# Prenorm attention with a two-layer local transformer branch: local scores in blocks of 64 queries by 128 keys, and one set of output transposes

## The reference

```
h = shift_token(x)                  # second half of the features comes from the token before
q, k, v = split(h @ wqkv)           # 8 heads of 64
q, k = l2norm(q) * qs, l2norm(k) * ks ; rotary embedding with a scale, q also times 8
# queries in blocks of 64; block w sees the keys of blocks w - 1 and w
mask = (i < j) | (i > j + 64) | (j == -1)
o = softmax(q k^T, masked) @ v
x = x + o @ wo
h = layernorm(shift_token(x)) * lg + lb
x = x + ((a * gelu(g)) @ w2 + b2)   # a, g = split(h @ w1 + b1), 341 features each
```

## Time and profile before

| | us |
|---|---|
| median of 3 runs | 3053.88 |
| lowest and highest | 3053.64, 3055.64 |
| the profiled execution's own time | 3055.99 |
| its span, first to last instruction | 3054.2 |
| busy in it: TensorE matmuls (PE) | 2986.4 (98%) |
| VectorE (DVE) | 1993.5 (65%) |
| ScalarE (ACT) | 1662.5 (54%) |
| GpSimd (POOL) | 1014.3 (33%) |

### The profile page before, as it was taken

How to read it: one execution, slowest core, us unless ns; L and a number is a source line. 1 busy time by engine, 2 the same in 40 slices (tenths; PEclk the granted TensorE clock), 3 DMA queues, 4 the chain that set the end, 5 groups by cost and what they waited for, 6 DMA issues and landing times.

```text
span 3054.2 us, 87852 instructions
## 1 busy us (share of the span) xinstructions
PE 2986.4 (98%) x34560; PEld 2067.3 (68%) x34560; DVE 1993.5 (65%) x6942; ACT 1662.5 (54%) x3126; POOL 1014.3 (33%) x987
## 2 busy tenths in 40 slices
PE   7999999999999999999999999999999999999999
PEld 5667666666767667676766767677676666766766
DVE  5576675757666665767657666666666756667564
ACT  4555555555555555555555555455555555555554
POOL 4143251515244240524405143141442414324030
PEclk9999999999999999999999999999999999999999
DMA  3000000000000000000000000000000000000000
GB/s 99 2 9 2 12 2 2 12 2 12 2 12 2 2 12 2 12 2 1 12 2 12 2 12 2 2 12 2 12 2 12 2 2 12 2 9 2 2 9 5
DMA packets 41791, 25.18 MB, mean 8 GB/s; under 512 B 13059, under 2 KB 40621, under 8 KB 41389
## 3 DMA queue, kind: packets, MB, share of 16 engines
q1 hardware_dynamic: 41388, 19.56, 2.3%
HBM read 14.96 MB, written 4.19 MB: 6 GB/s over the span
## 4 chain that ended last, share of the span: by engine, by line
PE 89%; DVE 4%; ACT 2%; POOL 2%; issue 1%; DMA 0%; SPq 0%; POOLq 0%; DVEq 0%; ACTq 0%
PE bank L1163 10%; PE bank L1117 9%; PE bank L1034 7%; PE bank L1207 7%; PE bank L1149 5%; PE bank L1223 4%; PE bank L1192 4%; PE bank L1175 4%; PE bank L1212 3%; PE bank L1141 3%; PE bank L1027 3%; PE bank L1245 3%; PE bank L1250 3%; PE bank L1028 3%; PE bank L1029 3%; PE bank L1255 2%
## 5 line engine op out<-in xcount | busy, mean ns | idle before, releaser
L890 DVE CUSTOM_DVE_ANT_0 bank<-bank,future 128x128 f32<-128x128 f32 (+3 forms) x1024 | 467.2, 527 | 92.2 <-PE bank L1076 91.9
L903 DVE CUSTOM_DVE_ANT_0 bank<-bank,band 128x192 f32<-128x192 f32 x1024 | 331.3, 395 | 219.2 <-PE bank L1094 219.0
L695 POOL TENSOR_TENSOR rnorm<-ssc,minus_half 128x8 f32<-128x8 f32 x256 | 426.8, 1667 | 21.3
L761 ACT ACTIVATE probs<-bank 128x512 f32<-128x512 f32 (+1 forms) x768 | 346.4, 532 | 153.3 <-PE bank L1126 153.0
L1117 PE MATMUL bank<-Qa,Ka 64*128 64x512 f32 (+3 forms) x2048 | 389.0, 462 | 9.4 <-ACT negT L753 4.3
L693 POOL TENSOR_SCALAR ssc<-ss 128x8 f32<-128x8 f32 x256 | 99.7, 390 | 866.6 <-DVE ss L948 861.8
L1163 PEld LDWEIGHTS bank<-Va,probs 128*64 128x64 f32 x10240 | 314.6, 137 | 47.7 <-issue 35.7
L1163 PE MATMUL bank<-Va,probs 128*64 128x65 f32 x10240 | 337.5, 223 | 0.6 <-ACT lprobs L769 0.6
L769 ACT ACTIVATE lprobs<-bank 128x384 f32<-128x384 f32 x512 | 221.9, 489 | 202.6 <-PE bank L1151 190.9
L792 ACT ACTIVATE scratch<-bank 128x512 f32<-128x512 f32 x256 | 153.3, 599 | 322.9 <-PE bank L1207 200.8
L941 DVE TENSOR_TENSOR scratch<-bank,rope_t 128x512 f32<-128x512 f32 x256 | 176.4, 689 | 231.0 <-ACT scratch L792 212.0
(11 more groups left out here) (154 smaller groups left out, 6871.8 us busy)
## 6 DMA issues: line engine op xcount, KB each, us to landing
x_res<-in_L_attn_x SPq DMA_DIRECT2D x16, 256.0 KB, 3.2
x_rows<-in_L_attn_x SPq DMA_DIRECT2D x16, 256.0 KB, 3.7
out<-yT SPq DMA_DIRECT2D x16, 256.0 KB, 2.4
Lqkv<-in_L_ffn_wqkv SPq DMA_DIRECT2D x2, 768.0 KB, 4.8
rope_t<-in_rope SPq DMA_DIRECT2D x8, 128.0 KB, 4.8
Kf<-in_L_attn_W_qkv SPq DMA_DIRECT2D x1, 768.0 KB, 7.3
Qf<-in_L_attn_W_qkv SPq DMA_DIRECT2D x1, 768.0 KB, 9.0
Lw<-in_L_ffn_w SPq DMA_DIRECT2D x2, 341.0 KB
```

The costliest lines, as they stand in the source:

```text
L695: g.tensor_tensor(rnorm[s][:, :], ssc[:, :], minus_half[:, :], ALU.pow).then_inc(rnorm_ready.sem, 1)
L761: psum.raise_read(a.activation(probs[j][:, at:at + n], psum.bank(i, task, (u, j))[:, 0:n], ACT.Exp, scale=float(HEAD) ** -0.5), i, task, ( ...
L890: ins = v.tensor_tensor_reduce(psum.bank(i, task, (u, j))[:, at:at + n], psum.bank(i, task, (u, j))[:, at:at + n], future[:, SEQ - n:SEQ], ...
L903: ins = v.tensor_tensor_reduce(psum.bank(i, task, (u, j))[:, k * BAND:(k + 1) * BAND], psum.bank(i, task, (u, j))[:, k * BAND:(k + 1) * BAND],
```

## The change

1. `f_st` scores blocks of 64 queries against the 128 keys that they see, the block before and their own. `K_padded` has 64 columns of zeros before the keys, so that the first block has a block before it. One head's 8 blocks of 128 keys by 64 queries fill one bank of 512 columns. The mask is one bfloat16 matmul over the 512 columns (`ahead`), and one over the first 64 that masks the padded keys (`no_key`); the maximum is subtracted by one bfloat16 matmul over 512 (`masked_last`), which also brings the remaining part of the mask, with constants that negf now holds. ScalarE's exponentials are 2 of 512 columns.
2. `f_pv` has one float32 matmul for each block, contracting over the block's 128 keys. Even blocks need V shifted by 64 tokens: `V_shifted`, which ScalarE writes in f_v with up to two more copies of 64 partitions each.
3. `out`: VectorE adds aT to yT, then TensorE turns yT with four transposes.
4. norm writes in place, without h; the load of the next x_res waits for xt, and x_rows' load is issued before it.
5. GpSimd makes 54 constants, and VectorE waits for `halved` before the first f_max. `STEPS` has new costs, so `ORDER` is planned anew.

The diff, cut to its core:

```diff
@@ STEPS @@
-    "norm": [("dve", 2.0, (), (), ()), ("pool", 1.0, (0,), (), ()), ("dve", 1.4, (1,), (), ())],
+    "norm": [("sp", 4.0, (), (), ()), ("dve", 2.0, (0,), (), ()), ("pool", 1.0, (1,), (), ()), ("dve", 1.4, (2,), (), ())],
-    "f_v": [("pe", 0.87, (), (0,), ()), ("act", 0.62, (0,), (), (0,))],
+    "f_v": [("pe", 0.87, (), (0,), ()), ("act", 1.8, (0,), (), (0,))],
-    "f_st": both([1.09, 1.09]) + [("act", 0.5, (b // 2,), (), (b,)) for b in range(4)],
-    "f_pv": [("pe", 0.86, (), (0,), ()), ("dve", 0.65, (0,), (), (0,))],
+    "f_st": both([1.5]) + [("act", 0.62, (0,), (), (b,)) for b in range(2)],
+    "f_pv": [("pe", 0.64, (), (0,), ()), ("dve", 0.65, (0,), (), (0,))],
-    "out": [("pe", 1.82, (), (0,), ()), ("dve", 0.75, (0,), (), (0,))]}
+    "out": [("dve", 0.72, (), (), ()), ("pe", 0.48, (0,), (0,), ()), ("dve", 0.75, (1,), (), (0,))]}
@@ sync @@
-            norm_ready.wait(sp, 0, ("norm",), "n")
+            psum.wait_filled(sp, 0, ("xt",), "x")
             load(x_res[:, :, :], slice(1, 2), x_loaded)
             for i in range(BATCH):
-                if i + 2 < BATCH:
-                    norm_ready.wait(sp, i + 1, ("norm",), "n")
-                    load(x_res[:, :, :], slice(i + 2, i + 3), x_loaded)
                 psum.wait_read(sp, i - 1 if i else None, ("out",), "t")
                 load(x_rows[:, :, :], slice(i, i + 1), x_again)
+                if i + 2 < BATCH:
+                    psum.wait_filled(sp, i + 1, ("xt",), "x")
+                    load(x_res[:, :, :], slice(i + 2, i + 3), x_loaded)
@@ make_rest @@
-                const(g.memset(minus_ones[:, :], -1.0))
+                const(g.memset(below, 0.0))
+                select(below.rearrange("p (b n) -> p b n", n=BLOCK), ALU.is_ge, MASK_BAND, 0, [[0, BLOCKS], [1, BLOCK]], -1)
+                const(g.memset(no_key[:, :], MASK_BAND))
+                const(g.memset(masked_last[:, :], 0.0))
+                for part in HALF:
+                    select(masked_last[:, 0:HEAD], ALU.not_equal, MASK_ROW, -part.start, [[-1, HEAD]], 1)
+                    select(masked_last[:, :], ALU.not_equal, -1.0, 1 - part.stop, [[0, P]], 1)
+                for part in K_padded:
+                    const(g.memset(part[:, 0:BLOCK], 0.0))
+                for part in V_shifted:
+                    const(g.memset(part[:, 0, :, :], 0.0))
+                    const(g.memset(part[:, :, :, HEAD:HEAD + 1], 1.0))
...
+                    select(negf[b][:, :, :].rearrange("p t (j r) -> p (t j) r", j=2), ALU.is_ge, MASK_BAND, 0, [[0, 2 * TILES], [1, HEAD]], -1)
@@ scalar, f_st @@
-                    for u in range(2):
-                        for j in range(2):
-                            psum.wait_filled(act, i, task, (u, j))
-                            psum.raise_read(a.activation(
-                                lprobs[j][:, 2 * u:2 * u + 2, 0:BAND],
-                                psum.bank(i, task, (u, j))[:, 0:2 * BAND].rearrange("p (t n) -> p t n", t=2), ACT.Exp), i,
-                                task, (u, j))
+                    for j in range(2):
+                        psum.wait_filled(act, i, task, (0, j))
+                        psum.raise_read(a.activation(lprobs[j][:, :], psum.bank(i, task, (0, j))[:, :], ACT.Exp), i, task, (0, j))
@@ scalar, f_v @@
-                    psum.raise_read(a.activation(Vf[task[1]][:, task[2], :, 0:HEAD], heads(psum.bank(i, task, "v")), ACT.Copy), i, task, "v")
+                    _, l, t = task
+                    bank = heads(psum.bank(i, task, "v"))
+                    a.activation(V_shifted[l][HALF[1], t, :, 0:HEAD], bank[HALF[0]], ACT.Copy)
+                    if t + 1 < TILES:
+                        a.activation(V_shifted[l][HALF[0], t + 1, :, 0:HEAD], bank[HALF[1]], ACT.Copy)
+                    psum.raise_read(a.activation(Vf[l][:, t, :, 0:HEAD], bank, ACT.Copy), i, task, "v")
@@ vector @@
-                            psum.wait_filled(dve, before_it(i, task, ("out",)), ("out",), "t")
+                            sum_ready.wait(dve, before_it(i, task, ("out",)), ("out",), "s")
...
                 elif kind == "out":
+                    psum.wait_read(dve, i, ("f_down", DEPTH - 1), "w")
+                    psum.wait_read(dve, i, ("a_out", PAIRS - 1), "u")
+                    v.tensor_tensor(yT[:, :], yT[:, :], aT, ALU.add).then_inc(sum_ready.sem, 1)
@@ tensor, f_st: the lines L1137 to L1154 give way to @@
+                    bank = psum.claims(pe, i, task, [(0, j) for j in range(2)], after)
+                    for j in range(2):
+                        mm(bank[j][:, :], row_of[HALF[j], 1, :], ahead[HALF[j], :], start=True, stop=False)
+                    for j in range(2):
+                        mm(bank[j][:, 0:BLOCK], row_of[HALF[j], 0, :], no_key[HALF[j], :], start=False, stop=False)
+                    for b in range(BLOCKS):
+                        keys = slice(p * SEQ + b * BLOCK, p * SEQ + (b + 2) * BLOCK)
+                        queries = slice(b * BLOCK, (b + 1) * BLOCK)
+                        for j in range(2):
+                            mm(bank[j][:, queries], K_padded[l][HALF[j], keys], Qf[l][HALF[j], p, queries],
+                               start=False, stop=False)
+                    last = [mm(bank[j][:, :], masked_last[HALF[j], :], negfT[p % 2][HALF[j], :], start=False, stop=True)
+                            for j in range(2)]
@@ tensor, f_pv: the lines L1173 to L1180 give way to @@
+                    for b in range(BLOCKS):
+                        t = b // 2
+                        V = (Vf if b % 2 else V_shifted)[l]
+                        ins = mm(bank[HALF[b % 2], t * (HEAD + 1):(t + 1) * (HEAD + 1)], lprobs[j][:, b * BLOCK:(b + 1) * BLOCK],
+                                 V[:, t, 2 * p + j, :], start=True, stop=True)
@@ tensor, out @@
-                    bank = psum.claim(pe, i, task, "t", [(("f_down", DEPTH - 1), "w")])
-                    for t in range(TILES):
-                        mm(bank[:, tile(t)], aT[:, tile(t)], ident[:, :], start=True, stop=False)
-                        ins = mm(bank[:, tile(t)], yT[:, tile(t)], ident[:, :], start=False, stop=True)
-                    psum.raise_filled(ins, i, task, "t")
+                    sum_ready.wait(pe, i, task, "s")
+                    transposes(i, task, "t", lambda t: yT[:, tile(t)])
```

More of the change, by code:

```diff
@@ L30 @@
 BAND = P + WINDOW
+BLOCK = WINDOW
+BLOCKS = SEQ // BLOCK
 QK_SCALE = 8.0
@@ L190, in holds @@
             ("f_q", 4): [("f_k", 6)], ("f_k", 5): [("f_q", 6)], ("f_q", 6): [("f_qt", 0)], ("f_k", 6): [("f_kt", 0)],
-            ("a_st", 3): [("a_pv", 0)], ("f_st", 2): [("f_pv", 0)], ("a_ot", 1): [("a_out", 0)]}.get((kind, k), [])
+            ("a_st", 3): [("a_pv", 0)], ("f_st", 1): [("f_pv", 0)], ("a_ot", 1): [("a_out", 0)]}.get((kind, k), [])
 LAST_OF = {kind: len(steps) - 1 for kind, steps in STEPS.items()}
@@ L227, in trial @@
             if engine == "pe":
-                change = CHANGE if k == 0 and TILING.get(task[0]) != self.tiling else 0.0
+                change = CHANGE if (k == 0 or task[0] == "out") and TILING.get(task[0]) != self.tiling else 0.0
                 idle += t + change - engines["pe"]
@@ L439, in prenorm_attention_and_local_transformer @@
         later_k = sb("later_k", [P, P], BF16)
-        outside = sb("outside", [P, 2, 3, BAND], BF16)
-        minus_ones = sb("minus_ones", [P, P], BF16)
+        ahead = sb("ahead", [P, SEQ], BF16)
+        no_key = sb("no_key", [P, BLOCK], BF16)
+        masked_last = sb("masked_last", [P, P], BF16)
         minus_first = sb("minus_first", [P, P], BF16)
@@ L516, in prenorm_attention_and_local_transformer @@
             a_max=[(u, j) for u in range(3) for j in range(2)], f_max=[(u, j) for u in range(2) for j in range(2)],
-            a_st=[(u, j) for u in range(3) for j in range(2)], f_st=[(u, j) for u in range(2) for j in range(2)],
+            a_st=[(u, j) for u in range(3) for j in range(2)], f_st=[(0, j) for j in range(2)],
             a_pv="v", f_pv="v"))
@@ L590, in _ @@
                     sp.dma_start(row_of[rows, k, :], mask_row[of, :]).then_inc(halved, 16)
-                    sp.dma_start(outside[rows, k, :, :], band[of, :, :]).then_inc(halved, 16)
                 sp.dma_start(later_k[rows, :], future_k[HEAD:P, :]).then_inc(halved, 16)
+                sp.dma_start(ahead[rows, :], below[0:BLOCK, :]).then_inc(halved, 16)
+            for part in negf:
+                sp.dma_start(part[BLOCK:P, :, :], part[0:BLOCK, :, :]).then_inc(halved, 16)
             weights(0)
@@ L748, in _ @@
                     p = task[-1]
-                    st, dst, u = ("a_st", negT, 2) if kind == "a_neg" else ("f_st", negfT, 1)
+                    st, dst, u = ("a_st", negT, 2) if kind == "a_neg" else ("f_st", negfT, 0)
                     j0, t0 = earlier(i, task, lambda t: t[0] == st and t[-1] % 2 == p % 2)
@@ L895, in _ @@
                     p = task[2]
+                    if i == 0 and task == ("f_max", 0, 0):
```

(18 more changed lines are left out.)

45 lines of the change are left out of this document (13 added, 32 removed).

## The result

The changed kernel takes 3155.15 us (median of 4 runs, 3151.19 to 3156.75) against 3054.76 us for before (4 runs): ratio 1.0326, 95% interval 1.0313 to 1.0339. It is **3.3% slower**, where the prediction gave 2957 us and slower a chance of 0.03. The profiled execution took 3154.7 us, its span is 3152.9.

What follows compares the result with a forecast made beforehand. PE's own instructions bound the kernel (98% busy). f_st +6, f_pv -89, out -23, the sum's wait +2, the end -1, ACT +3 and start +5 make -97 us: 2957 us, 80% range 2932 to 2996.

Steps and rivals of the forecast that it cites:

- waits: PE's waits in the new order: no term beyond ACT, the sum and the start; up to +15 us in the bounds.
- +3 for ACT: ScalarE: f_v copies +132 us, exponentials -69, busy about 1725, beside PE; +3 us taken from 0 to 38.
- +5 at the start: GpSimd's 15 more constants delay the first xT_lo and a_proj by 5.3 us (4 to 7).
- The sign of being wrong that I had named: ACT or DVE entries over 30 us among PE's waits would make the forecast wrong the slow way.
- Rival (b): New waits from an order planned with f_st 0.7 us too short: +25 to +75 us, 2985 to 3030; chance 0.11.
- f_st: Local scores, 128 times: 2.22 us becomes 2.25 to 2.27, passes at the load's 0.11; +6 us.
- Rival (a): f_st's score blocks pay as planned, passes at 0.065 us, f_st 1.55, 92 us less: 2865; chance 0.07.
- (d): In f_st a load waits for its own row group's matmul: f_st 3.12, 109 us more, 3066; chance 0.02.
- f_pv: 256 times: six slots of 0.058 us fall away from 0.96 us, 0.35 each; -89 us (bounds -67 to -101).
- out: 16 times 1.89 to 0.43 us, -23 us; PE's wait for the sum +2, 11 if fully exposed.
- rival (c): PE stands for ScalarE's f_v copies, 132 us on top: 3089; chance 0.02.
- x_res: Later load of the next x_res: nothing taken; without any cover about 4 us of DVE, 15 times.

Runs made afterwards that it cites:

- e2: The kernel before with the changed kernel's planner table, so its instructions run in the new order: 3188.3 us, ratio 1.0433 against before.
- e9: The changed kernel with its planner settings kept and only the prices of f_st (2.2) and f_pv (0.5) put right: 3184.3 us, ratio 1.0422 against before.
- e10: The changed kernel with its own prices (1.5, 0.64) and new planner settings (offsets 0, 1.4, 0.9, 1.2, spread 0.3, weight 0.1): 3003.1 us.
- e13: The kernel before with only the planner settings changed (offsets 0, 1.4, 0.9, 1.2, spread 0.3, weight 0.1): 3062.0 us, ratio 1.0023 against before.
- e1: The changed kernel with the old planner table, so its instructions run in the order of before: 3073.7 us, ratio 1.0061 against before.
- e8: e7 with VectorE's sum issued as soon as both of its parts are written: 2993.9 us, ratio 0.9798 against before.
- e4: The changed kernel in its own order without ScalarE's copies into V_shifted, even blocks taking the unshifted V: 3135.42 us, ratio 1.0261 against before.
- e11: e8 with the 12 constants only the local scores need made last, and the first xT_lo not waiting for them: 2987.8 us, ratio 0.978 against before.
- e12: e11 with other planner settings (offsets 0, 1.4, 1.1, 1.5, spread 0.4, weight 0.1): 2986.0 us, ratio 0.9772 against before.
- e5: e1 with the eight matmuls of out in place of the sum and transposes: 3041.6 us, ratio 0.9955 against before.
- e6: e1 with VectorE's sum kept but issued as soon as both of its parts are written: 3033.7 us, ratio 0.9929 against before.
- e7: The changed kernel replanned with f_st 2.2 and f_pv 0.5 and new settings (offsets 0, 1.4, 0.9, 1.2, spread 0.3, weight 0.1): 2996.6 us, ratio 0.9807.

## Why the prediction was wrong

**The failed step: waits.** The sum has +3 for ACT, +2 for the sum's wait and +5 at the start, and lets the rest of the new order cost nothing. Measured are +140 us of PE idle time, some 130 more than the sum had, and about 50 of lower clock; with 15 us less work saved than forecast, that is the distance from the forecast's span of 2957 to the measured 3153. I took the 68 us of idle time of before as a property of the kernel, because PE was "98% busy" and the other engines had 35% or more to spare. e2 shows that it is one of the order: same instructions, same engines, 132 us more, and 158 us of idle time for 68. The sign of being wrong that I had named, an ACT or DVE entry over 30 us, did not show either: the largest entry of after is 18.6, and the loss lies in many small ones and in the tail.

**Rival (b)** had the right name, new waits from the new order, at 0.11. It was undersized (+25 to +75) and its mechanism fell. It blamed the short price of f_st: e9 puts the price right and is 29 us worse, e10 leaves it wrong and takes 152 us off. I had read `least_idle`'s arguments and not asked how steep the time is in them. No trace of before shows that; the one second plan of the old kernel that was run does not either, since e13 moves it by 6 us. Replaying the orders through the planner's own model would have been a warning: with right prices for f_st and f_pv it ends after's order at 3145 with 348 us of idle PE, and before's, with before's prices, at 3098 with 190. With the short f_st of `STEPS` it says 3067 and has the wrong sign. Its times are not the chip's (it puts e1 at 3147, measured 3074), so it warns and does not forecast.

**The clock** had no term at all. At 0.998 in before it seemed constant; after has 0.982.

**f_st: right.** +8 us measured (start to next task's start, summed over 128 tasks: 286.9 in before, 294.9 in e8) for +6. Rival (a), score blocks at 0.065 a pass, and (d), a load that waits for its own row group (0.163), both fall on the 0.114 of the rows above.

**f_pv: right alone, 12 us short in all.** 235.6 us became 158.7 in e8, -77 for -89. One that stands alone fell from 0.96 to 0.62, as said (0.61); here from e8's timeline:

```profile
1542.52 0.27 PE L1206 MATMUL bank<-V_shifted,lprobs 128*64 128x65 f32 x1
...
1542.98 0.22 PE L1206 MATMUL bank<-Vf,lprobs 128*64 128x65 f32 x1
1543.14 0.40 PE L1137 MATMUL bank<-identb,neg 128*128 128x128 bf16 x4
```

But 0.96 was the wrong price for all 256: 47 of them in before stand beside an a_pv, which splits the columns in the same way, and cost 0.81, so that the mean was 235.6/256 = 0.92. The row I had picked was a lone one. These are times to the next task's start, and 8 of e8's 158.7 us are PE waiting in front of that task (1 in before).

**out**: 1.89 to 0.49, -22 us over 16 for -23. Its wait for the sum, sized +2, is 14.1 us in after, 45.4 in e1, under 4 once it is issued early. The bound I had named, 11 us exposed, was not a bound: the sum queues on VectorE behind other tasks, up to 7.8 us, and not for 0.7 alone.

**ACT**: 1713.3 busy for a forecast 1725. The sum took the old exponentials as busy time (221.9, in which neighbours overlap) and the new ones as 256 full lengths; as busy time they fell by 83 us (139.0 in after), not 69. In after 20 us of the copies are exposed by e4, for 3. It is inside the 0 to 38 that I gave, and rival (c), 132 us on top, is ruled out by e4.

**x_res**, priced at nothing: no wait of its own. VectorE waits for its load once, at the start, 3.7 us in after and 3.5 in before.

**Start**: the first wait for xT_lo 14.5 for 8.6, +5.9 for +5.3; e11 confirms it.

In sum: at full clock PE's work fell by 90.6 us (2895.8 busy in e8 against 2986.4) for the forecast's 106. With a fitting plan, the early sum and the start mended the kernel is at 2986 (e12), 29 above the forecast and inside its 80% range. Of the 27 us between e12's span and the forecast's 2957, 18 are work of PE (87.5 us saved for 106) and 9 idle time beyond what the sum had.

**What stays open**: why these settings serve the old costs and not the new. The traces show how the bad orders differ. In us, the time from norm's start on VectorE to xt's copy on ScalarE for one sequence, and the time from the last attention matmul to the end of the span:

| runs | norm to xt | attention's end to span's end |
|---|---|---|
| after, e2, e4, e9 | 6 to 19 from the second sequence on | 123 to 131 |
| before, e1, e5, e6, e7, e8, e10, e11, e12, e13 | 6 to 28 in the second sequence, 107 to 190 from the eighth on | 17 to 33 |

The four runs of the first row are the four above 3100 us. In their orders norm and xt stay close, and the last layer stands alone at the end. That is seen in all runs; whether it makes the waits is argued, not tested. Offsets, spread and weight were changed together in all runs, and every new plan that came out good has the weight 0.1. In the planner's own model with right prices, the weight alone (0.1 for 0.05) takes e9's order from 3199 us to 3090 and lets norm and xt drift apart; the offset alone gives 3169 with the two still close, and the spread alone changes nothing. No run has them apart.

## What to carry to other kernels

Where a static order over all engines was tuned, an edit of the instructions is two changes, and the order must be measured apart: run the new instructions in the old order, and the old ones in the new. Task prices read from start-to-start distances held within 0.06 us here (f_st 2.28 for 2.25 to 2.27, a lone f_pv 0.62 for 0.61, `out` 0.49 for 0.43), but the sign came from 140 us of waits that no engine's busy share announced, so re-tune the plan's settings before judging the edit. The float32 score matmuls of 64 columns went at the pace of their weight loads (0.114 us a pass-pair), so narrower blocks saved nothing on that side; the gain was all in the fewer products of f_pv and out.

## What the hardware showed that I had not expected

In after's last stretch, with eight waits of PE of 1.7 to 3.7 us in the 50 us shown below, the granted clock was at times at the lower of its two levels, 1.2 of 2.4 GHz: 0.50 over 3082 to 3098 us, 1.00 over 3055.7 to 3058. After, over 3050 to 3100 us:

```profile
3050.00:3100.00 50.00, 27.19 (x158) 16.08 (x160) 20.14 (x64) 16.08 (x27) 27.52 (x26) 0.65 0.00 1
```

The mean of 0.65 is a mix of the two levels. The order with 140 us more idle time lost another 50 or so in matmuls that ran slower, and got them back with the idle time. Of the 57 us of clock worked out above, which are an upper bound, 31 lie in the last 153 us (0.20 of 153). By the profiled executions, after, e1, e2, e4 and e9, with 158 to 216 us idle, have mean clocks of 0.980 to 0.993, and the other nine kernels, before among them, with under 130 us idle, all have 0.997 or more. The total is not all of it: e1 and e2 idle for 160 and 158 us, and have 0.993 and 0.985.
